# Grouped convolution ahead of a feed-forward network: 16 places in, 8 out, both parts of the weights in one stationary

## The chip, the cores and the metric

The kernel runs on one core of a Trainium2 chip. The metric is the device time of one execution in microseconds; the number given for a kernel is the median of its runs.

## The reference, cut to what matters

```
# x: 128 x 32 x 512, f32 (samples, channels, places)
out = conv_general_dilated(x, weight,          # weight: 32 x 8 x 9
        padding=[(4, 4)], feature_group_count=4)
h = out + einsum('nd,od->no', c, c_weight)[:, :, None] + bias[None, :, None]
xt = h.reshape(-1, 512)
y = (silu(xt @ W_gate.T) * (xt @ W_up.T)) @ W_down.T   # W: 1376 x 512, 512 x 1376
return x + y.reshape(x.shape)
```

The 32 channels form four groups of eight. A convolution with nine taps runs over the 512 places inside each group, and then every (sample, channel) row of 512 places goes through the gated network.

## The kernel before

**The work.** The four channel groups g = 0 to 3 are done one behind the other. For each there are two stages. The first makes gate and up for the 1376 hidden units, in eleven slices f = 0 to 10 of 128 (the last of 96), by seven products for each slice (a scheme of sums and differences of halves, so that seven take the place of eight). The second, `down`, multiplies the gated values by W_down, in 22 units for each group. f32 values are kept as two parts, hi (rounded to fp32r) and lo (the rest), and every product of two f32 matrices is three matmuls: hi by hi, lo by hi, hi by lo. A product of the first stage has two halves q of its 256 terms, so it is six matmuls of 512 columns.

**The convolution of group g + 1 runs inside the first stage of group g**, one step k = 0 to 7 for each slice (group 0's own convolution stands ahead of everything). A block is 16 places of 8 channels, 128 rows with the samples as columns; a step does four blocks, 512 columns. An output block of 16 places needs its own block of inputs and eight places of the next, so two stationaries hold the taps as banded matrices: `ta` (own block) and `tb` (the next one's part), each with hi and lo: six matmuls a step, in one PSUM bank, and ahead of them a head of three matmuls of 128 columns.

For the groups 1 to 3, which the change touches, a step goes through the engines thus (`lag(g)` is 1 for g = 0, so k = f - 1 there, and k = f later; line numbers are those of the profile):

- SyncE loads 128 places of x into `x_in` in eight transfers (L355), at k = 1, 3, 5, and at the end for the next group.
- VectorE turns 32 x 32 blocks into `x_blk` (`turn_x`, L1138), ahead of `gate_a`.
- ScalarE makes `xt_hi` (`split_x`, L859 is its helper), VectorE `xt_lo` (L1091 is its helper).
- TensorE multiplies, one iteration later and behind product 3 (`conv_step`, L640 and L645; `conv_head`, L631, behind product 1 at k = 1).
- VectorE adds `ctxb` and writes to `win` (`read_conv`, L1192; `read_head`, L1182), behind `prepare` and ahead of `up_b`.
- SyncE sends the four windows of the step from `win` to `stage` (`stage_step`, L344), in the next iteration. An even step's read waits until the two steps before it are out of `win` (`staged`).

**The order of the work is written out by hand**: each engine has its own loop over g and f, and semaphores tie them. Inside a slice TensorE goes 1, 2, 3, 4, 0 of the next slice, 5, 6 (L727). Products 0, 2, 4 and 5 collect in the same PSUM bank, so each waits until the one before has been copied by ScalarE (`copy_chain`; product 5 waits for `copied4`). Product 6 waits until VectorE has added product 3 (`up_b`, L1260), product 3 of the next slice for `up_a` (L1265), product 1 for `gate_a` (L1255). The products `gated` are L1274 and L1278.

In group 0 the weights are prepared on the way (`prepare`): TensorE transposes them (L654, L665), VectorE makes T1 and T2, differences of weights (L1164, L1168), GpSimd T3 and T4 (L522, L523), and ScalarE (L859), VectorE (L1091) and GpSimd (L530) split them into hi and lo in `ring`, from where SyncE saves them. ScalarE's queue holds `copy_chain(n, f, 4)` behind `prepare(f + 1, 2)`, the splits of T1 and T2:

```
                    if more:
                        prepare(f + 1, 1)
                    if more:
                        prepare(f + 1, 2)
                    copy_chain(n, f, 4)
```

Groups 1 to 3 load the saved weights again (L404), and there is no `prepare`.

Of the kernel before, what the change touches and what calls it, by code (L numbers as in the profile page):

```python
# [11 lines left out]
P = 128  # L12


def adaln_ffn(nc, x, cond, bias, conv_w, ctx_w, w_gate, w_up, w_down, out):
# [8 lines left out]
    WB = 4  # L24
# [77 lines left out]
    with ExitStack() as ctx:  # L102
# [24 lines left out]
        x_in = sb("x_in", [P, CG, P])  # L127
        x_blk = sb("x_blk", [P, WB, R, CG])
# [4 lines left out]
        ta_hi = sb("ta_hi", [P, P], F32R)  # L133
        ta_lo = sb("ta_lo", [P, P], F32R)
        tb_hi = sb("tb_hi", [P, P], F32R)
        tb_lo = sb("tb_lo", [P, P], F32R)
        ident = sb("ident", [P, P])

        copy0, copy2, copy4, act_a, act_b = (mix[:, n, :] for n in range(5))

# [65 lines left out]
        x_turned = sem("x_turned")  # L206
        xt_hi_done = sem("xt_hi_done")
# [88 lines left out]
        def x_place(grp, i):  # L296
            return x_first[:, i - 1] if grp == 0 and i > 0 else x_in[:]
# [13 lines left out]
        x_turn = x_blk[:, :, :, :].rearrange("n b r c -> n (b r c)")  # L311

        def x_split_from(grp, k):
            return xt_bank(grp, k)[:] if grp == 0 else x_turn
# [35 lines left out]
        def _(sp):  # L350
            def load_x(grp, i):
                if grp > 0:
                    for quad in range(NB):
                        for c in range(CQ):
                            sp.dma_start(x_in[quad * QUAD:(quad + 1) * QUAD, c::CQ, :],  # L355
                                         x[:, grp * CG + quad * CQ + c, i * P:(i + 1) * P].rearrange("(b n) l -> n b l", b=NB)
                                         ).then_inc(x_loaded, LD)
                    return
# [130 lines left out]
        def _(pool):  # L489
# [42 lines left out]

            def mix_h_first(q):
# [15 lines left out]
            pool.tensor_copy(reorder[:].rearrange("p (m r) -> p m r", r=R), ident[:].rearrange("p (r m) -> p m r", r=R)).then_inc(consts, 1)  # L549
            wrap(1)  # L550
# [4 lines left out]
            for g in range(G):  # L555
                for f in range(FC):
                    if g == 0 and f + 2 < FC:
                        wrap(f + 2)
                    if g == 0 and f + 1 < FC:
                        mix_t(f + 1)  # L560
                        mix_t_lo(f + 1)

        @block.tensor
        def _(pe):
# [56 lines left out]
            def conv_head(grp):  # L621
# [8 lines left out]
                for n, (t, v) in enumerate(terms(tb_hi, tb_lo, *xt(grp))):  # L630
                    mm = pe.matmul(conv_ps[:, 0:P], t[:], v[:, 0:P], start=n == 0, stop=n == 2)  # L631
# [187 lines left out]
            for g in range(G):  # L819
# [3 lines left out]
                for f in range(1 if g == 0 else 0, FC):  # L823
# [33 lines left out]
        def _(act):  # L857
# [3 lines left out]
            def split_toep(grp):  # L861
# [4 lines left out]
                if grp == 1:  # L866
# [3 lines left out]
                    act.wait_ge(toep_done, 3)  # L870
                hi(ta_hi[:], toep[:, grp:grp + 1, HALO:QN, :])
                hi(tb_hi[:, TB0:P], toep[:, grp:grp + 1, 0:HALO, :]).then_inc(t_hi_done, 1)

# [168 lines left out]
            for g in range(G):  # L1042
# [3 lines left out]
                for f in range(1 if g == 0 else 0, FC):  # L1046
# [7 lines left out]
                    if conv and 0 <= k < STEPS:  # L1054
# [6 lines left out]
                    silu_a(n, f)  # L1061
                    if n == 1:
# [26 lines left out]
        def _(dve):  # L1089
# [26 lines left out]
            def split_toep(grp):  # L1116
# [4 lines left out]
                if grp == 0:  # L1121
# [4 lines left out]
                    lo(t[2][:, R - HALO:, :], in_bank[0][:, 0:HALO, :], t[3][:, R - HALO:, :]).then_inc(t_lo_done, 1)  # L1126
                else:
# [3 lines left out]
            def turn_x(grp, k):  # L1131
# [5 lines left out]
                l0 = k % 2 * WB * R  # L1137
                dve.transpose(x_turn, x_in[:, :, l0:l0 + WB * R].rearrange("p m (w r) -> p w m r", r=R)).then_inc(x_turned, 1)  # L1138
# [40 lines left out]
            def read_head(grp):  # L1179
                dve.wait_ge(ctx_done, 1 if grp == 0 else 2)  # L1180
                dve.wait_ge(conv_done, CPG * grp + 1)
                dve.tensor_tensor(head[HEAD0:P, :], conv_ps[HEAD0:P, 0:P], ctxb[HEAD0:P, grp, :],  # L1182
                                  ALU.add).then_inc(conv_out, 1)

            def read_conv(grp, k):
# [8 lines left out]
                if k == STEPS - 1:  # L1194
# [3 lines left out]
                    last = dve.tensor_copy(to[HEAD0:P, JJ - 1, :], head[HEAD0:P, :])  # L1198
                last.then_inc(conv_out, 1)
# [132 lines left out]
            for g in range(G):  # L1332
                conv = g + 1 < G
                for f in range(1 if g == 0 else 0, FC):
# [3 lines left out]
                    if conv and 0 <= k < STEPS:  # L1338
# [68 lines left out]
```

## Time and profile before

| what | value |
|---|---|
| runs | 750.9 us median of 3 (750.73 to 751.24) |
| profiled execution | 751.72 us |
| its span | 749.9 us, granted clock 0.999 |
| TensorE matmul busy | 739.6 us, 99% |
| VectorE busy | 379.5 us, 51% |
| ScalarE busy | 274.4 us, 37% |
| GpSimd busy | 52.4 us, 7% |
| group 0's first stage, with the conv of group 1 | 48 to 164 us |
| first stages of groups 1 and 2, with a conv | 228 to 348 and 405 to 524 us |

The page lists the busy time of each engine, the span in 40 slices, the chain of work that ended last, and the groups of instructions. A matmul is shown with its full passage (some 390 ns for 512 columns), while the next one starts sooner, so the busy share of TensorE says little; what counts is the distance from one start to the next.

### The profile page before, as it was taken

How to read it: one execution, taken by the hardware profiler on the slowest of the kernel's cores; microseconds unless marked ns; L12 is line 12 of the kernel's file. 1: busy time of each engine (PE TensorE's matmuls, PEld its weight loads, DVE VectorE, ACT ScalarE, POOL GpSimd, SP SyncE). 2: the span in 40 equal slices, each digit the busy share in tenths (PEclk: the TensorE clock that was granted, in tenths of full speed). 3: DMA queues.
4: the chain of work that ended last, by engine and by line, in shares of the span. 5: the costliest groups of instructions: out<-in, count | busy, mean ns of one | idle time of the engine just before them, and what ended most of it. 6: DMA issues, size and time to landing. Idle time of an engine off the chain costs nothing.

```text
span 749.9 us, 10087 instructions
## 1 busy us (share of the span) xinstructions
PE 739.6 (99%) x3375; PEld 602.4 (80%) x3375; DVE 379.5 (51%) x639; ACT 274.4 (37%) x521; POOL 52.4 (7%) x88
## 2 busy tenths in 40 slices
PE   7999999999999999999999999999999999999998
PEld 6778888878888888887888888887888888887886
DVE  3896766654765454436734545443753333334224
ACT  4565655543433233234322333324431332333221
POOL 4433323210000000000000000000000000000000
PEclk9999999999999999999999999999999999999999
DMA  6496578569977677765544866866443967775413
GB/s 186 114 317 239 187 273 281 186 226 327 354 268 247 216 222 219 197 205 159 167 135 171 282 202 193 244 194 180 162 133 106 312 190 196 194 193 172 141 29 112
DMA packets 115029, 152.37 MB, mean 203 GB/s; under 512 B 12482, under 2 KB 50530, under 8 KB 114978
## 3 DMA queue, kind: packets, MB, share of 16 engines
q1 hardware_dynamic: 114496, 151.51, 64.8%
q8 instruction: 28, 0.46, 0.2%
q10 hardware_dynamic: 482, 0.21, 0.1%
q14 instruction: 23, 0.19, 0.1%
HBM read 108.95 MB, written 34.34 MB: 191 GB/s over the span
## 4 chain that ended last, share of the span: by engine, by line
PE 94%; DVE 2%; DMA 1%; SPq 1%; issue 1%; ACT 1%; POOL 0%; POOLq 0%; DVEq 0%
PE bank L727 55%; PE bank L790 32%; PE bank L645 3%; PE bank L640 3%; SPq L344 1%; PE bank L683 1%; DVE hc_lo L1091 1%; DMA x_in<-in_x 1%; PE bank L606 1%; PE bank L654 1%; PE bank L665 0%; DMA stage<-g_all 0%; DVE g_all L1294 0%; DVE ring L1091 0%; DVE g_all L1192 0%
## 5 line engine op out<-in xcount | busy, mean ns | idle before, releaser
L727 PE MATMUL bank<-hc_hi,ring 128*128 128x512 f32 (+1 forms) x1204 | 374.0, 392 | 1.0 <-issue 1.0
L727 PEld LDWEIGHTS bank<-hc_hi,ring 128*128 128x128 f32 (+1 forms) x1204 | 221.4, 185 | 50.2 <-issue 1.4
L727 PE MATMUL bank<-hc_lo,ring 128*128 128x512 f32 (+1 forms) x602 | 234.8, 390 | 0.0
L790 PE MATMUL bank<-ring,g_hi 128*128 128x512 f32 (+1 forms) x704 | 218.6, 392 | 0.0
L790 PEld LDWEIGHTS bank<-ring,g_hi 128*128 128x128 f32 (+1 forms) x704 | 131.2, 188 | 28.1 <-DVE g_lo L1091 0.8
L859 ACT ACTIVATE mix<-bank 128x512 f32<-128x512 f32 (+1 forms) x129 | 76.7, 594 | 188.0 <-PE bank L727 188.0
L790 PE MATMUL bank<-ring,g_lo 128*128 128x512 f32 (+1 forms) x352 | 137.1, 390 | 0.0
L727 PEld LDWEIGHTS bank<-hc_lo,ring 128*128 128x128 f32 (+1 forms) x602 | 111.5, 185 | 25.8
L1091 DVE TENSOR_TENSOR g_lo<-g_all,g_hi 128x512 fp32r<-128x512 f32 (+1 forms) x88 | 60.4, 689 | 88.6 <-ACT g_hi L859 88.6
L859 ACT ACTIVATE g_hi<-g_all 128x512 fp32r<-128x512 f32 (+1 forms) x88 | 55.1, 629 | 114.1 <-PE bank L790 114.0
L1265 DVE TENSOR_TENSOR mix<-bank,mix 128x512 f32<-128x512 f32 (+1 forms) x43 | 29.7, 691 | 129.4 <-PE bank L727 129.4
L790 PEld LDWEIGHTS bank<-ring,g_lo 128*128 128x128 f32 (+1 forms) x352 | 66.1, 188 | 13.9
L1260 DVE TENSOR_TENSOR mix<-bank,mix 128x512 f32<-128x512 f32 (+1 forms) x43 | 29.6, 688 | 71.1 <-ACT mix L859 71.1
L981 ACT ACTIVATE mix<-bank 128x512 f32<-128x512 f32 (+1 forms) x43 | 25.7, 598 | 43.3 <-PE bank L727 43.3
L859 ACT ACTIVATE xt_hi<-x_blk 128x512 fp32r<-128x512 f32 (+1 forms) x33 | 17.0, 540 | 65.2 <-DVE x_blk L1138 65.2
L1091 DVE TENSOR_TENSOR hc_lo<-stage,hc_hi 128x512 fp32r<-128x512 f32 x50 | 32.9, 696 | 0.9 <-ACT hc_hi L859 0.8
L1255 DVE TENSOR_TENSOR mix<-bank,mix 128x512 f32<-128x512 f32 (+1 forms) x43 | 28.9, 671 | 7.1 <-PE bank L727 4.7
L859 ACT ACTIVATE hc_hi<-stage 128x512 fp32r<-128x512 f32 x50 | 28.6, 618 | 3.2 <-DMA stage<-g_all 3.1
L1274 DVE TENSOR_TENSOR g_all<-mix 128x512 f32<-128x512 f32 (+1 forms) x43 | 29.5, 686 | 0.0
L1278 DVE TENSOR_TENSOR g_all<-mix 128x512 f32<-128x512 f32 (+1 forms) x43 | 29.3, 682 | 0.0
L1192 DVE TENSOR_TENSOR win<-bank,ctxb 128x512 f32<-128x512 f32 (+1 forms) x24 | 16.1, 671 | 25.0 <-PE bank L645 23.2
L975 ACT ACTIVATE mix<-mix 128x512 f32<-128x512 f32 (+1 forms) x43 | 26.7, 621 | 0.0
(141 smaller groups left out, 468.7 us busy)
## 6 DMA issues: line engine op xcount, KB each, us to landing
ring<-saved SPq DMA_DIRECT2D x319, 256.0 KB, 3.0
saved<-ring SPq DMA_DIRECT2D x99, 256.0 KB, 3.7
g_all<-in_x SPq DMA_DIRECT2D x32, 256.0 KB, 3.6
out_y<-g_all SPq DMA_DIRECT2D x32, 256.0 KB, 3.7
x_in<-in_x SPq DMA_DIRECT2D x96, 64.0 KB, 2.1
stage<-win SPq DMA_DIRECT2D x96, 64.0 KB, 2.9
w_nat<-in_L_ffn_W_gate SPq DMA_DIRECT2D x10, 256.0 KB, 3.4
w_nat<-in_L_ffn_W_up SPq DMA_DIRECT2D x10, 256.0 KB, 3.4
```

The costliest lines, as they stand in the source:

```text
L640: pe.matmul(bank[:], t[:], v[:, at:at + WB * P], start=n == 0, stop=False)
L727: mm = pe.matmul(bank[0:w, :], wt, hv, start=fresh and q == 0 and t == 0, stop=q == 1 and t == 2, skip_group_check=not fresh)
L790: mm = pe.matmul(acc(half, tt)[:], gs, wd, start=f == 0 and t == 0, stop=f == FC - 1 and t == 2)
L859: return act.activation(dst, src, ACT.Copy)
L975: act.activation(act_a[0:w], act_a[0:w], ACT.Silu).then_inc(silu_a_done, 1)
L981: act.activation(act_b[0:w], chain_ps[f % 2][0:w, :], ACT.Silu).then_inc(silu_b_done, 1)
L1091: return dve.tensor_tensor(dst, src, hi_part.bitcast(F32), ALU.subtract)
L1255: dve.tensor_tensor(act_a[0:w], second_ps[0:w, :], copy0[0:w], ALU.add).then_inc(gate_a_done, 1)
L1260: dve.tensor_tensor(copy4[0:w], third_ps[0:w, :], copy4[0:w], ALU.add).then_inc(up_b_done, 1)
L1265: dve.tensor_tensor(copy2[0:w], third_ps[0:w, :], copy2[0:w], ALU.add).then_inc(up_a_done, 1)
L1274: dve.tensor_tensor(g_all[0:w, f, 0, :], copy2[0:w], act_a[0:w], ALU.mult).then_inc(g_done[0], 1)
L1278: dve.tensor_tensor(g_all[0:w, f, 1, :], copy4[0:w], act_b[0:w], ALU.mult).then_inc(g_done[1], 1)
```

## The change

For groups 1 to 3 a block of 16 input places now gives only 8 output places. With 8 outputs of 8 channels, hi and lo of the band each take 64 columns of a stationary, so both fit in one: `pair_even` is hi then lo, `pair_odd` lo then hi. A matmul of it by `xt_hi` and one by `xt_lo` give all products; the result for one half of the outputs stands as two parts in the two halves of the partitions of a bank, which are added when they are read. A step of the same 64 output places needs eight input blocks, at distances of 8 places: 1024 columns, four matmuls of 512, in the two banks `conv_ps` and `xt_ps`. `x_in` gets a margin of eight places on both sides. Core of the diff:

```diff
-        x_in = sb("x_in", [P, CG, P])
-        x_blk = sb("x_blk", [P, WB, R, CG])
+        x_in = sb("x_in", [P, CG, HALO + P + HALO])
+        x_turn = sb("x_turn", [P, 2 * WB * P])
+        conv_t = sb("conv_t", [P, 4 * P], F32R)
+        PAIRED = 1
+        HALF = P // 2
+        pair_even, pair_odd = conv_t[:, 0:P], conv_t[:, HALF:HALF + P]
...
 (load_x)
+                    size = P + HALO if paired(grp) and i < KC - 1 else P
...
 (GpSimd)
+            def pad_x(grp):
+
+                pool.wait_ge(x_turned, STEPS * grp + STEPS - 2)
+                pool.memset(x_in[:, :, HALO + P:], 0.0).then_inc(x_padded, 1)
...
+                    if g + 1 < G and paired(g + 1) and f == STEPS - 1:
+                        pad_x(g + 1)
...
 (TensorE)
+                if paired(grp):
+                    for n, v in enumerate(xt(grp)):
+                        mm = pe.matmul(conv_ps[:, 0:P], pair_odd, v[:, 2 * WB * P:], start=n == 0, stop=n == 1)
...
+            def paired_step(grp, k):
+                pe.wait_ge(xt_lo_done, STEPS * grp + k + 1)
+                pe.wait_ge(conv_out, CPG * grp + k + 1)
+                for half, (bank, t) in enumerate(((conv_ps, pair_even), (xt_ps, pair_odd))):
+                    for n, v in enumerate(xt(grp)):
+                        mm = pe.matmul(bank[:], t, v[:, half * WB * P:(half + 1) * WB * P], start=n == 0, stop=n == 1)
+                mm.then_inc(conv_done, 1)
...
                     product(g, f, 2)
+                    if conv and 1 <= k <= STEPS and paired(g + 1):
+                        paired_step(g + 1, k - 1)
                     product(g, f, 3)
-                    if conv and 1 <= k <= STEPS:
+                    if conv and 1 <= k <= STEPS and not paired(g + 1):
                         conv_step(g + 1, k - 1)
...
 (ScalarE)
+            def split_pairs(grp, k):
+                act.wait_ge(conv_done, CPG * grp + (k + 1 if k > 0 else 0))
+                act.wait_ge(x_turned, STEPS * grp + k + 1)
+                last = hi(xt_hi[:, 0:2 * WB * P], x_turn[:])
...
-                    if conv and 0 <= k < STEPS:
+                    if conv and 0 <= k < STEPS and not paired(g + 1):
                         split_x(g + 1, k)
...
                     copy_chain(n, f, 2)
                     silu_a(n, f)
+                    if conv and 0 <= k < STEPS and paired(g + 1):
+                        split_pairs(g + 1, k)
...
 (VectorE, turn_x)
+                for half in range(2 if paired(grp) else 1):
+                    at = l0 + half * HALO
+                    last = dve.transpose(x_turn[:, half * WB * P:(half + 1) * WB * P],
+                                         x_in[:, :, at:at + WB * R].rearrange("p m (w r) -> p w m r", r=R))
...
+            def split_pairs(grp, k):
+                dve.wait_ge(xt_hi_done, STEPS * grp + k + 1)
+                last = lo(xt_lo[:, 0:2 * WB * P], x_turn[:], xt_hi[:, 0:2 * WB * P])
...
 (read_head)
+                    rows = slice(HEAD0 - HALF, HALF)
+                    dve.tensor_tensor(head[HEAD0:P, :], conv_ps[rows, 0:P], ctxb[rows, grp, :], ALU.add).then_inc(conv_lo_out, 1)
+                    dve.wait_ge(conv_lo_out, (2 * STEPS + 2) * (grp - PAIRED) + 1)
+                    dve.tensor_tensor(head[HEAD0:P, :], conv_ps[HEAD0:P, 0:P], head[HEAD0:P, :], ALU.add).then_inc(conv_out, 1)
...
+            def read_pairs(grp, k):
+                i = k // 2
+                if k % 2 == 0:
+                    dve.wait_ge(staged[(i - 1) % KC], STAGED * (grp if i == 0 else grp + 1))
+                dve.wait_ge(conv_done, CPG * grp + k + 2)
+                lower, upper = slice(0, HALF), slice(HALF, P)
+                halves = ((conv_ps, lower, upper), (xt_ps, upper, lower))
+                w0 = k % 2 * WB
+                to = [windows(grp, i)[mine, w0:w0 + WB, :] for _, mine, _ in halves]
+                for n, (bank, mine, other) in enumerate(halves):
+                    dve.tensor_tensor(to[n], bank[other, :].rearrange("p (w n) -> p w n", w=WB),
+                                      ctxb[other, grp:grp + 1, :].broadcast_to([HALF, WB, P]), ALU.add).then_inc(conv_lo_out, 1)
+                for n, (bank, mine, other) in enumerate(halves):
+                    dve.wait_ge(conv_lo_out, (2 * STEPS + 2) * (grp - PAIRED) + 2 * k + n + 2)
+                    last = dve.tensor_tensor(to[n], bank[mine, :].rearrange("p (w n) -> p w n", w=WB), to[n], ALU.add)
...
-                    if conv and 0 <= k < STEPS:
+                    if conv and 0 <= k < STEPS and (k == 0 or not paired(g + 1)):
                         turn_x(g + 1, k)
...
                         split_toep(g + 1)
+                    if conv and 1 <= k <= STEPS and paired(g + 1):
+                        read_pairs(g + 1, k - 1)
                     if conv and 0 <= k < STEPS:
-                        split_x(g + 1, k)
+                        (split_pairs if paired(g + 1) else split_x)(g + 1, k)
...
-                    if conv and 1 <= k <= STEPS:
+                    if conv and 1 <= k <= STEPS and not paired(g + 1):
                         read_conv(g + 1, k - 1)
                     up_b(n, f)
...
+                    if conv and 0 <= k < STEPS - 1 and paired(g + 1):
+                        turn_x(g + 1, k + 1)
                     up_a(n, f)
```

VectorE's queue in one iteration of group 0, before the change, from `turn_x` to the last `gated`. `ring` holds weights, `t_all` T1 and T2, `win` the windows of the convolution.

```order
L1138 STREAM_TRANSPOSE x_blk<-x_in 128x512 [waits xt_lo_done,x_loaded]
L1255 TENSOR_TENSOR mix<-bank,mix 128x512 [waits g_a_done,copied0,product_done1]
L1091 TENSOR_TENSOR ring<-x_gate,ring 128x256 [waits w_hi_done] x2
L1091 TENSOR_TENSOR xt_lo<-x_blk,xt_hi 128x512 [waits xt_hi_done]
L1091 TENSOR_TENSOR ring<-bank,ring 128x256 [waits w_hi_done]
L1164 TENSOR_TENSOR t_all<-bank,x_gate 128x256
L1168 TENSOR_TENSOR t_all<-bank,t_all 128x256 [waits t4_done,t1_done]
L1091 TENSOR_TENSOR ring<-t_all,ring 128x256 [waits w_hi_done] x2
L1192 TENSOR_TENSOR win<-bank,ctxb 128x512 [waits conv_done,staged0]
L1260 TENSOR_TENSOR mix<-bank,mix 128x512 [waits copied4]
L1265 TENSOR_TENSOR mix<-bank,mix 128x512 [waits product_done6]
```

The same place after the change, from `gate_a` (L1352) to `up_a` (L1362):

```order
L1352 TENSOR_TENSOR mix<-bank,mix 128x512 [waits g_a_done,copied0,product_done1]
L1141 TENSOR_TENSOR ring<-x_gate,ring 128x256 [waits w_hi_done] x2
L1287 TENSOR_TENSOR win<-bank,ctxb 64x512 [waits conv_done,staged0]
L1287 TENSOR_TENSOR win<-bank,ctxb 64x512
L1291 TENSOR_TENSOR win<-bank,win 64x512 [waits conv_lo_out] x2
L1141 TENSOR_TENSOR xt_lo<-x_turn,xt_hi 128x1024 [waits xt_hi_done]
L1141 TENSOR_TENSOR ring<-bank,ring 128x256 [waits w_hi_done]
L1234 TENSOR_TENSOR t_all<-bank,x_gate 128x256
L1238 TENSOR_TENSOR t_all<-bank,t_all 128x256 [waits t4_done,t1_done]
L1357 TENSOR_TENSOR mix<-bank,mix 128x512 [waits copied4]
L1199 STREAM_TRANSPOSE x_turn<-x_in 128x512 [waits xt_lo_done,x_loaded]
L1362 TENSOR_TENSOR mix<-bank,mix 128x512 [waits product_done6]
```

The reads of the convolution moved from behind T1 and T2 to ahead of them, and became four; the split became twice as long; the transposes (two, of which one is shown) moved from ahead of `gate_a` to between `up_b` and `up_a`, one step early.

TensorE's queue in group 0, from the end of product 4 to product 6, after the change. `product_done`, `copied4` and `up_b_done` are what the products wait for.

```order
L687 MATMUL bank<-ident,w_nat 128x128 [waits gate_kept,nat_wrapped]
L760 MATMUL bank<-hc_hi,ring 128x512 [waits silu_b_done,w_made0]
L760 MATMUL bank<-hc_hi,ring 128x512 [waits copied4,w_made5]
L698 MATMUL bank<-ident,w_nat 128x128 [waits t2_done,nat_wrapped]
L760 MATMUL bank<-hc_hi,ring 128x512 [waits up_b_done,w_made6]
```

Nothing moved here: of each product the first row is shown (0 of the next slice, 5, 6), with its waits as before. What moved on TensorE is the convolution step, from behind product 3 to ahead of it.

## Rows read from the trace of the kernel before

**Rows 1.** The page: busy time, share of the span and instructions of each engine.
```profile
PE 739.6 (99%) x3375; PEld 602.4 (80%) x3375; DVE 379.5 (51%) x639; ACT 274.4 (37%) x521; POOL 52.4 (7%) x88
```

**Rows 2.** The chain that ended last, in order of time: start us, us, what.
```profile
94.94 5.47 PE bank L727 x24
...
131.00 5.49 PE bank L727 x24
...
347.55 57.40 PE bank L790 x252
```

**Rows 3.** Timeline, group 0, f = 1: start us, us, engine, instruction [idle before].
```profile
54.53 0.42 DVE L1164 TENSOR_TENSOR t_all<-bank,x_gate 128x256 f32<-128x256 f32 x1
...
56.52 0.71 PE L727 MATMUL bank<-hc_hi,ring 128*128 128x512 f32 x2 [0.95 <-issue]
```

**Rows 4.** Timeline, group 0, f = 5: VectorE, and SyncE's windows.
```profile
96.36 0.69 DVE L1265 TENSOR_TENSOR mix<-bank,mix 128x512 f32<-128x512 f32 x1 [3.54 <-PE bank L727]
96.97 0.68 DVE L1278 TENSOR_TENSOR g_all<-mix 128x512 f32<-128x512 f32 x1
...
101.11 0.42 DVE L1091 TENSOR_TENSOR ring<-bank,ring 128x256 fp32r<-128x256 f32 x1 [0.20 <-ACT ring L859]
101.45 0.41 DVE L1164 TENSOR_TENSOR t_all<-bank,x_gate 128x256 f32<-128x256 f32 x1
101.90 0.42 DVE L1168 TENSOR_TENSOR t_all<-bank,t_all 128x256 f32<-128x256 f32 x1
...
106.23 2.49 SPq L344 DMA_DIRECT2D stage<-win  x4
```

**Rows 5.** Timeline of TensorE, group 0: starts of product 1 (f = 5), 5, next 1.
```profile
96.16 0.62 PE L727 MATMUL bank<-hc_hi,ring 128*128 128x512 f32 x2
...
105.05 0.62 PE L727 MATMUL bank<-hc_hi,ring 128*128 128x512 f32 x2
...
108.27 0.40 PE L727 MATMUL bank<-hc_hi,ring 128*128 128x512 f32 x1
```

**Rows 6.** Groups by line and form, VectorE: busy us, mean ns | idle before.
```profile
L1138 DVE STREAM_TRANSPOSE x_blk<-x_in 128x512 f32<-128x512 f32 x24 | 16.9, 705 | 0.0
L1091 DVE TENSOR_TENSOR xt_lo<-x_blk,xt_hi 128x512 fp32r<-128x512 f32 x24 | 16.5, 689 | 3.5 <-ACT xt_hi L859 3.4
...
L1192 DVE TENSOR_TENSOR win<-bank,ctxb 128x512 f32<-128x512 f32 x21 | 14.4, 687 | 19.8 <-PE bank L645 18.0 <-DMA stage<-win 1.8
...
L1091 DVE TENSOR_TENSOR xt_lo<-x_blk,xt_hi 128x128 fp32r<-128x128 f32 x9 | 2.6, 285 | 0.0
...
L1182 DVE TENSOR_TENSOR head<-bank,ctxb 32x128 f32<-32x128 f32 x4 | 1.2, 296 | 1.2 <-PE bank L631 1.1
```

**Rows 7.** Line 344, the windows issued at 262 us: ns, starts, and landing.
```profile
L344 SPq DMA_DIRECT2D stage<-win x4: 553/594/600, 261.9 to 263.8; - x4
...
DMA to landing us min/median/max: 2.7/3.0/3.3
```

**Rows 8.** The page's DMA issues, loads of x: KB each, median us to landing.
```profile
x_in<-in_x SPq DMA_DIRECT2D x96, 64.0 KB, 2.1
```

**Rows 9.** Timeline of VectorE, group 0, f = 2, around the head's read.
```profile
62.46 0.66 DVE L1255 TENSOR_TENSOR mix<-bank,mix 128x512 f32<-128x512 f32 x1
63.14 0.30 DVE L1182 TENSOR_TENSOR head<-bank,ctxb 32x128 f32<-32x128 f32 x1
63.47 0.42 DVE L1091 TENSOR_TENSOR ring<-x_gate,ring 128x256 fp32r<-128x256 f32 x1
```

**Rows 10.** Line 344, the windows issued at 106.2 us.
```profile
DMA to landing us min/median/max: 2.4/2.6/2.7
```

**Rows 11.** Timeline, group 1, step 2: start of product 1, and the read.
```profile
261.34 0.61 PE L727 MATMUL bank<-hc_hi,ring 128*128 128x512 f32 x2
...
267.07 0.69 DVE L1192 TENSOR_TENSOR win<-bank,ctxb 128x512 f32<-128x512 f32 x1 [1.56 <-PE bank L645]
```

**Rows 12.** Line 344, the windows issued at 272.8 us.
```profile
DMA to landing us min/median/max: 3.7/3.9/4.0
```

More of the change, by code:

```diff
@@ L296, in x_place @@
         def x_place(grp, i):
-            return x_first[:, i - 1] if grp == 0 and i > 0 else x_in[:]
+            return x_first[:, i - 1] if grp == 0 and i > 0 else x_in[:, :, HALO:HALO + P]
         def blocks(grp, k):
@@ L310, in adaln_ffn @@
         NB, CQ = P // QUAD, CG // (P // QUAD)
-        x_turn = x_blk[:, :, :, :].rearrange("n b r c -> n (b r c)")
         def x_split_from(grp, k):
-            return xt_bank(grp, k)[:] if grp == 0 else x_turn
+            return xt_bank(grp, k)[:] if grp == 0 else x_turn[:, 0:WB * P]
         def xt_at(grp, k):
@@ L629, in conv_head @@
                     pe.wait_ge(conv_out, CPG * grp)
-                for n, (t, v) in enumerate(terms(tb_hi, tb_lo, *xt(grp))):
-                    mm = pe.matmul(conv_ps[:, 0:P], t[:], v[:, 0:P], start=n == 0, stop=n == 2)
+                if paired(grp):
+                    for n, v in enumerate(xt(grp)):
+                        mm = pe.matmul(conv_ps[:, 0:P], pair_odd, v[:, 2 * WB * P:], start=n == 0, stop=n == 1)
+                else:
+                    for n, (t, v) in enumerate(terms(tb_hi, tb_lo, *xt(grp))):
+                        mm = pe.matmul(conv_ps[:, 0:P], t[:], v[:, 0:P], start=n == 0, stop=n == 2)
+                mm.then_inc(conv_done, 1)
[5 more added lines that the diff above has]
+                        mm = pe.matmul(bank[:], t, v[:, half * WB * P:(half + 1) * WB * P], start=n == 0, stop=n == 1)
                 mm.then_inc(conv_done, 1)
@@ L870, in split_toep @@
                     act.wait_ge(toep_done, 3)
+                if paired(grp):
+                    for at in (0, P):
+                        last = hi(conv_t[:, at:at + HALF], toep[:, grp:grp + 1, HALO:2 * HALO, :])
+                    last.then_inc(t_hi_done, 1)
+                    return
                 hi(ta_hi[:], toep[:, grp:grp + 1, HALO:QN, :])
                 hi(tb_hi[:, TB0:P], toep[:, grp:grp + 1, 0:HALO, :]).then_inc(t_hi_done, 1)
+            def split_pairs(grp, k):
+                act.wait_ge(conv_done, CPG * grp + (k + 1 if k > 0 else 0))
+                act.wait_ge(x_turned, STEPS * grp + k + 1)
+                last = hi(xt_hi[:, 0:2 * WB * P], x_turn[:])
+                if k == 0:
+                    last = hi(xt_hi[:, 2 * WB * P:], head[:])
+                last.then_inc(xt_hi_done, 1)
             def split_x(grp, k):
@@ L1198, in read_conv @@
                     last = dve.tensor_copy(to[HEAD0:P, JJ - 1, :], head[HEAD0:P, :])
+                last.then_inc(conv_out, 1)
+            def read_pairs(grp, k):
[13 more added lines that the diff above has]
+                    last = dve.tensor_tensor(to[n], bank[mine, :].rearrange("p (w n) -> p w n", w=WB), to[n], ALU.add)
+                if k == STEPS - 1:
+                    last.then_inc(conv_lo_out, 1)
+                    dve.wait_ge(conv_lo_out, (2 * STEPS + 2) * (grp - PAIRED + 1))
+                    last = dve.tensor_copy(windows(grp, i)[HEAD0:P, JJ - 1, :], head[HEAD0:P, :])
                 last.then_inc(conv_out, 1)
```

33 lines of the change are left out of this document (25 added, 8 removed).

## The prediction

> **What bounds the kernel now.** The page comes first: TensorE is busy for 739.6 of 749.9 us, VectorE for 51%, ScalarE for 37% [rows 1]. Busy matmuls are pipelined, so I look next at whether TensorE ever waits. The chain of waits in order of time is one row of products behind the other: 252 matmuls in 57.40 us, 0.228 us for each matmul of 512 columns, with no gap [rows 2]. So a product (six matmuls) takes 1.37 us, and a matmul taken away is worth 0.228 us where nothing else is late. Two stretches matter. The eight conv steps of channel group 1 run during group 0's products f = 1 to 9, where iterations are 12.0 us apart (three of them in 131.00 - 94.94 = 36.06 us [rows 2]). Those of groups 2 and 3 run during the products of groups 1 and 2, where an iteration is 48 matmuls, 10.93 us. Then I read one iteration of each kind, on VectorE, ScalarE and TensorE together. The reader should see in it what TensorE takes from VectorE: product 5 needs the copy of product 4, and that copy stands on ScalarE's queue behind the splits of T1 and T2, which VectorE makes. In f = 1 this wait already shows: T1 starts at 54.53, product 5 at 56.52 after 0.95 us of idle TensorE, so product 5 starts **1.99 us after T1** when T1 is late [rows 3]. In a normal iteration T1 starts at 101.45, so the copy would allow 103.44, and product 5 starts at 105.05, when its turn comes [rows 4, 5]. T1 has 1.6 us of slack.
>
> **What the change takes from TensorE.** Columns per group before: head 3 x 128, seven steps of 6 x 512, one of 3 x 512 + 3 x 384, together 24576. After: 2 x 128 + 32 x 512 = 16640. The difference, 7936 columns at 0.228 us per 512, is 3.53 us per group and 10.6 us in all. The page will count 17 matmuls fewer per group (51 - 34).
>
> **What it adds on VectorE**, per step. One read of 687 ns becomes four, each of 64 partitions but as many columns. A transpose of 705 ns becomes two. The split of 512 columns (689 ns) becomes one of 1024: the slope between 128 columns (285) and 512 (689) is 1.05 ns per column, so 1.23 us, and 1.14 until the next can start [rows 6]. By throughput alone that fits: about 3 us more in 11.5. What counts is the place. The four reads and the long split now stand ahead of T1, T2 and up_b; before, the one read stood behind T1 and T2. Beside other work lie:
> - the two transposes, 1.3 us between up_b and up_a, where VectorE now waits 3.54 us for product 6 [rows 4]; if that idle time went, they would cost it in full;
> - the loads they read. They are asked for in the same place of SyncE's queue, behind the four windows. In groups 1 and 2 those are issued by 3.1 us after product 1 begins; eight more issues at the windows' 0.62 end by 8.1, and landing takes 2.1 [rows 7, 8]: 10.2, just ahead of the transposes, which begin at 10.4 in those iterations by the count below;
> - ScalarE's split, of the same columns, which runs beside the reads and would have to exceed 2.7 us to hold VectorE;
> - GpSimd's four small memsets. One of them stands in f = 7 behind GpSimd's splits, and VectorE's last transposes wait for it, in the same idle time.
>
> **What a read costs.** Neighbours start 0.61 us apart although each lasts 0.69 (96.36, 96.97 [rows 4]). The new reads cross from one half of the partitions to the other, alternately, which before never does. Bounds: 0.35 if half the partitions cost half the time, 0.61 as neighbours do, 0.72 if each waits until the one in front is finished. The nearest row is the head's read, the one instruction that starts at another partition than its neighbours. It starts at 63.14, after the end of the one in front (62.46 + 0.66), and the next starts at 63.47, after its own end [rows 9]. So I take 0.69 + 0.03 = **0.72**, four reads 2.88. Against half the time speaks the head's 296 ns on 32 partitions beside 285 on 128, both of 128 columns [rows 6].
>
> The Trainium skill has a rule for this ("VectorE: DVE Perf Modes", section "Two Vector instructions with no wait between them"): an instruction whose input or output starts in another group of 32 partitions than the last one's is held until all earlier ones have finished. By that rule a read is 0.72, without it 0.61, and the sum below would be 759.6; rows 9 agree with the rule.
>
> **Group 0, one iteration**, counted from the start of product 1. Products 1 and 2 end at 2.73, the four new matmuls at 3.64. VectorE sees the end of a product 0.20 after TensorE has gone on (96.16 and 96.36 [rows 4, 5]), so the reads run from 3.84 to 6.72, the split to 7.86; one short operation (0.34, from 101.11 to 101.45 [rows 4]), and T1 starts at 8.20. Product 5 follows at 10.19. Before, it started 8.89 after product 1 (105.05 - 96.16), now it could at some 8.4. From its start to the next product 1 are 3.22 us (108.27 - 105.05 [rows 5]). So the iteration takes 13.4 us, not 12.0: **+1.4**, with the saving already in it. The others differ from it:
> - Steps 2, 4 and 6 also wait until the windows of the step before have left `win`. SyncE issues these 4.33 us after T2's start (101.90, 106.23 [rows 4]), here 0.45 before product 1 begins; the last goes 1.9 later [rows 7] and lands after 2.6 [rows 10]: near 4.1, so +0.25, in all +1.65.
> - In f = 2 the head comes first. VectorE's two adds, 0.33 each, end at 3.35; the four matmuls start at 3.40, not 2.85, and T1 at 8.86: 14.1 against 12.3 (its iteration held the head before too), +1.8.
> - f = 9 has a read but no split: 12.5 against 11.85, +0.7.
> - f = 1 has no read, but three transposes and a split of 1152 columns on both engines, T1 1.4 later; it was late already, so all of it counts: +1.4.
>
> Sum: 1.4 + 1.8 + 3 x 1.4 + 3 x 1.65 + 0.7 = **+13.0**.
>
> **Groups 1 and 2, each.** There is no T1; product 6 needs up_b. Odd steps: reads to 6.72, split to 7.86, up_b done at 8.55, and product 6 starts at 9.11 (46 matmuls less its own six): no wait. Steps 2, 4 and 6 wait for the windows. SyncE issues them behind the refills of the ring, from 261.9 to 263.8, they land 3.0 later [rows 7], and VectorE's read starts at 267.07, 5.73 after product 1 began at 261.34 [rows 11]. That was when the conv's matmuls were done anyway; now they are done 1.9 earlier and the windows are late next: 5.73 + 2.88 + 1.14 + 0.69 + 0.10 (handing over) = 10.54 against 9.11, 1.4 us of idle TensorE, three times. The head costs 0.55 as above. So -3.53 + 0.55 + 4.2 = **+1.2**, twice: +2.4.
>
> **Sum:** 13.0 + 2.4 = +15.4 on the profiled execution's 751.7. That one stands 0.8 above the median of the runs, 750.9, so the forecast is 750.9 + 15.4 = **766.3 us**, slower.
>
> **Rivals.**
> - *Neighbours' pitch:* the reads cost 0.61. Reads and split together are then 0.48 shorter, eight times in group 0 and six times later, 6.7 us: 759.6. Rows 9 speak against it.
> - *The other side, cheap half reads:* at 0.35 four reads take 1.4 and T1 starts at 6.72, product 5 at 8.71, an iteration 11.9 against 12.0. Group 0: 1.4 + 0.3 - 0.3 + 0.45 - 0.5 = +1.3. Later up_b is done at 9.06, before 9.11: -3.0 per group. In all -4.7: 746.2, faster. It decides from where four reads take less than about 1.9 us. The head's 296 ns speak against it; that no row shows 64 partitions, for it.
> - *Late windows:* one burst of the same transfers landed after 3.9 [rows 12]. If all six of groups 1 and 2 do, each costs 0.9 more: +5.4, 771.7. For it: the moved timing meets other refills. Against: one of group 1's seven bursts did it, by the same view.
> - *All hidden:* only the matmuls count, 740.3. It would need the reads to stand behind T1, and they don't.
>
> **How the numbers follow.** The forecast's own case gets 0.60 (761 to 770: 0.3 us either way in each of 14 waits), neighbours' pitch 0.22, late windows 0.11, cheap reads or all hidden 0.05, a wash 0.02. The likeliest gives 766.3; the range 757 to 772 takes in the second and third case. A measurement here tells 0.2%, 1.5 us, from no change: faster 0.05, same 0.02, slower 0.93.
>
> **What would show it.** TensorE idle ahead of product 5 in f = 1 to 9 (1.5 to 2 us each) and ahead of product 6 in three iterations of groups 1 and 2; T1 near 8.2; iterations of 13.4 and 13.65; the reads 0.72 apart. Reads 0.35 or 0.61 apart, T1 before 6.4, or no idle time ahead of product 6 would prove that step wrong. The whole fails if VectorE's queue is short of work where I count it full.

## The result and the profile after

| what | before | after |
|---|---|---|
| median of the runs beside each other | 751.07 us (6 runs, 750.32 to 751.78) | 770.51 us (6 runs, 769.15 to 773.53) |
| profiled execution, its span | 751.72, 749.9 us | 770.19, 768.2 us |

The ratio is 1.026, with an interval of 1.0246 to 1.0274: slower, by 19.4 us where 15.4 were forecast. The time lies inside the range of 757 to 772.

The page of the changed kernel, busy times, the slices of two engines, and the groups on VectorE (out<-in, count | busy us, mean ns | idle before, and for what); they answer to [rows 1, 6]:

```profile
PE 732.9 (95%) x3324; PEld 593.8 (77%) x3324; DVE 458.6 (60%) x729; ACT 282.2 (37%) x515; POOL 52.3 (7%) x92
...
PE   8988878889999999999999999999999999999998
...
DVE  4897888865485777763854678764663333334224
...
L1287 DVE TENSOR_TENSOR win<-bank,ctxb 64x512 f32<-64x512 f32 x48 | 33.1, 689 | 28.1 <-DMA stage<-win 14.4
...
L1291 DVE TENSOR_TENSOR win<-bank,win 64x512 f32<-64x512 f32 x48 | 33.1, 689 | 1.1
L1141 DVE TENSOR_TENSOR xt_lo<-x_turn,xt_hi 128x1024 fp32r<-128x1024 f32 x24 | 29.4, 1226 | 6.7 <-ACT xt_hi L894 6.1
```

TensorE has its 51 matmuls fewer (3375 - 3324) and is busy for 95% of the span, not 99%. A slice is 19.2 us; but for the last one, the slices below 9 stand in the first 173 us, where group 0's first stage is. VectorE is 79 us busier. The reader should compare 33.1 + 33.1 us for the reads with the 14.4 of one read a step (21 of 24 steps) [rows 6]: a read of 64 partitions takes 689 ns, as one of 128 did (687).

What TensorE now waits for, from the view of waits (engine, line, what for: us in total, times, longest):

```profile
PE bank L760 <- ACT mix L894: 15.4, 8, 2.1
PE bank L760 <- DVE mix L1357: 6.2, 6, 1.3
PE bank L760 <- issue: 2.6, 1, 2.6
...
PE bank L664 <- DVE head L1256: 1.7, 3, 0.6
```

Three of the forecast's waits stand here in order. Product 5 waits for ScalarE's copy in f = 2 to 9, eight times, and in f = 1 once more (the 2.6 that the view puts down to issue). Product 6 waits for `up_b` six times, in groups 1 and 2. The conv's matmuls wait three times for the head. Together 25.9 us, of which only the 0.95 of f = 1 was there before [rows 3].

VectorE in one iteration of group 0, f = 3, whose product 1 starts on TensorE at 77.48 (timeline: start us, us, engine, instruction, idle before):

```profile
79.70 0.69 DVE L1352 TENSOR_TENSOR mix<-bank,mix 128x512 f32<-128x512 f32 x1
80.31 0.75 DVE L1141 TENSOR_TENSOR ring<-x_gate,ring 128x256 fp32r<-128x256 f32 x2
81.32 1.41 DVE L1287 TENSOR_TENSOR win<-bank,ctxb 64x512 f32<-64x512 f32 x2 [0.26 <-PE bank L664]
82.76 1.39 DVE L1291 TENSOR_TENSOR win<-bank,win 64x512 f32<-64x512 f32 x2
84.18 1.23 DVE L1141 TENSOR_TENSOR xt_lo<-x_turn,xt_hi 128x1024 fp32r<-128x1024 f32 x1
85.44 0.42 DVE L1141 TENSOR_TENSOR ring<-bank,ring 128x256 fp32r<-128x256 f32 x1
85.78 0.41 DVE L1234 TENSOR_TENSOR t_all<-bank,x_gate 128x256 f32<-128x256 f32 x1
```

and TensorE, where product 1 starts, where product 5 starts, and where the next product 1 does:

```profile
77.48 0.62 PE L760 MATMUL bank<-hc_hi,ring 128*128 128x512 f32 x2
...
87.82 0.70 PE L760 MATMUL bank<-hc_hi,ring 128*128 128x512 f32 x2 [1.98 <-ACT mix L894]
...
91.11 0.62 PE L760 MATMUL bank<-hc_hi,ring 128*128 128x512 f32 x2
```

Counted from product 1: reads at 3.84, split at 6.70, T1 at 8.30, product 5 at 10.34. Four reads take 84.18 - 81.32 = 2.86 us. The next product 1 starts at 91.11, after 13.63 us.

Group 1, step 2, whose product 1 starts at 277.68, on VectorE:

```profile
283.26 1.41 DVE L1287 TENSOR_TENSOR win<-bank,ctxb 64x512 f32<-64x512 f32 x2 [2.66 <-DMA stage<-win]
284.70 1.39 DVE L1291 TENSOR_TENSOR win<-bank,win 64x512 f32<-64x512 f32 x2
286.12 1.23 DVE L1141 TENSOR_TENSOR xt_lo<-x_turn,xt_hi 128x1024 fp32r<-128x1024 f32 x1
287.38 0.69 DVE L1357 TENSOR_TENSOR mix<-bank,mix 128x512 f32<-128x512 f32 x1
```

on TensorE:

```profile
288.22 0.70 PE L760 MATMUL bank<-hc_hi,ring 128*128 128x512 f32 x2 [1.30 <-DVE mix L1357]
```

and the burst of windows that the read waits for, by line 356 (instructions, durations in ns, first and last start), where the answering rows are [rows 7]:

```profile
L356 SPq DMA_DIRECT2D stage<-win x4: 552/595/600, 278.2 to 280.1; - x4
...
DMA to landing us min/median/max: 3.1/3.2/3.5
```

The last window, issued at 280.1, lands some 3.2 later, and the read starts at 283.26, 5.58 after product 1. Product 6 starts 10.54 after it. That this is the forecast's number to the hundredth is luck: the read started 0.15 earlier than counted (5.58 for 5.73), and `up_b` 0.12 later behind the split (1.26 for 1.14). Of the six such waits this is the longest, 1.30 us; the six are 1.04 on average.

### Where the time went

`up_a` closes an iteration on VectorE. The distances between its starts, before and after:

| iteration | before | after | more | forecast |
|---|---|---|---|---|
| group 0, up to f = 1 | 60.02 | 62.91 | 2.9 | 1.4 |
| f = 2 | 12.33 | 14.77 | 2.4 | 1.8 |
| f = 3 to 8, mean of six | 11.97 | 13.66 | 1.7 | 1.4 and 1.65 |
| f = 9 | 10.79 | 11.91 | 1.1 | 0.7 |
| group 1 in all | 169.65 | 170.58 | 0.9 | 1.2 |
| group 2 in all | 176.57 | 177.35 | 0.8 | 1.2 |

Group 0 lost 16.6 us (166.91 to 183.51), groups 1 and 2 together 1.7: 18.3, the difference of the spans. The runs say 19.4: the execution profiled before stood 0.7 above its median and the one after 0.3 below.

The theory for the experiments is the prediction's: in group 0 the reads and the long split stand ahead of T1 on VectorE, and TensorE waits for what hangs on T1; in groups 1 and 2 the windows leave `win` too late. Rivals to be told apart: that VectorE and the DMA queues carry too much, wherever it stands; that the transfers in group 0 (SyncE saves weights there) hold it; and, for the reads, that their crossing from one half of the partitions to the other costs nothing.

### The profile page after: what moved, and what is told of

Read it like the earlier page. It is cut to its first block, busy times and chain, and to the rows that moved or that the text cites. A ratio compares the mean times of both kernels' runs of the same rounds, so it can differ in the third digit from the quotient of the medians.

```text
span 768.2 us, 10073 instructions
## 1 busy us (share of the span) xinstructions
PE 732.9 (95%) x3324; PEld 593.8 (77%) x3324; DVE 458.6 (60%) x729; ACT 282.2 (37%) x515; POOL 52.3 (7%) x92
## 4 chain that ended last, share of the span: by engine, by line
PE 78%; DVE 11%; DMA 3%; issue 3%; SPq 2%; ACT 2%; POOL 0%; DVEq 0%; ACTq 0%; POOLq 0%
PE bank L760 42%; PE bank L823 31%; DVE win L1287 3%; PE bank L664 2%; DMA stage<-win 2%; DVE xt_lo L1141 2%; SPq L356 2%; DVE win L1291 2%; DVE ring L1141 1%; ACT mix L894 1%; PE bank L716 1%; ACT ring L894 1%; DVE hc_lo L1141 1%; DMA x_in<-in_x 1%; DVE mix L1357 1%
## 5 line engine op out<-in xcount | busy, mean ns | idle before, releaser
L760 PE MATMUL bank<-hc_hi,ring 128*128 128x512 f32 (+1 forms) x1204 | 375.6, 393 | 24.3 <-ACT mix L894 15.4
L1362 DVE TENSOR_TENSOR mix<-bank,mix 128x512 f32<-128x512 f32 (+1 forms) x43 | 29.7, 690 | 85.2 <-PE bank L760 85.2
L1287 DVE TENSOR_TENSOR win<-bank,ctxb 64x512 f32<-64x512 f32 x48 | 33.1, 689 | 28.1 <-DMA stage<-win 14.4
L1352 DVE TENSOR_TENSOR mix<-bank,mix 128x512 f32<-128x512 f32 (+1 forms) x43 | 29.7, 690 | 8.3 <-PE bank L760 3.1
L1291 DVE TENSOR_TENSOR win<-bank,win 64x512 f32<-64x512 f32 x48 | 33.1, 689 | 1.1
L1141 DVE TENSOR_TENSOR xt_lo<-x_turn,xt_hi 128x1024 fp32r<-128x1024 f32 x24 | 29.4, 1226 | 6.7 <-ACT xt_hi L894 6.1
L894 ACT ACTIVATE ring<-t_all 128x256 fp32r<-128x256 f32 (+1 forms) x44 | 18.0, 413 | 38.9 <-DVE t_all L1234 31.7
L1199 DVE STREAM_TRANSPOSE x_turn<-x_in 128x512 f32<-128x512 f32 x48 | 30.9, 682 | 1.6 <-POOL x_in L549 1.6
```

Of the source, the lines that this page charges most:

```text
L760: mm = pe.matmul(bank[0:w, :], wt, hv, start=fresh and q == 0 and t == 0, stop=q == 1 and t == 2, skip_group_check=not fresh)
L894: return act.activation(dst, src, ACT.Copy)
L1141: return dve.tensor_tensor(dst, src, hi_part.bitcast(F32), ALU.subtract)
L1199: last = dve.transpose(x_turn[:, half * WB * P:(half + 1) * WB * P], x_in[:, :, at:at + WB * R].rearrange("p m (w r) -> p w m r", r=R))
L1287: dve.tensor_tensor(to[n], bank[other, :].rearrange("p (w n) -> p w n", w=WB), ctxb[other, grp:grp + 1, :].broadcast_to([HALF, WB, P]), AL ...
L1291: last = dve.tensor_tensor(to[n], bank[mine, :].rearrange("p (w n) -> p w n", w=WB), to[n], ALU.add)
```

## Experiments

**1. The new convolution for groups 2 and 3 alone, and for group 1 alone.** The places of the loss, apart.

```diff
-        PAIRED = 1
+        PAIRED = 2
```

> The new convolution for groups 2 and 3 alone; group 1's, which runs inside group 0's products, stays as before. If the loss comes from T1 standing behind the reads in group 0 (my theory, 16.6 us of the 18.3 between the two profiles), only the waits ahead of product 6 and the heads remain: 751.1 + 1.7 = 752.8 us (752 to 754). If the loss is simply VectorE's added work, wherever it stands, two thirds of 19.4 us remain: 764 us.

```diff
-            return grp >= PAIRED
+            return grp == PAIRED
```

> The complement: the new convolution for group 1 alone, groups 2 and 3 as before. T1's place: 751.1 + 16.6 = 767.7 us (766 to 770), with TensorE idle ahead of product 5 in f = 1 to 9. Added work wherever it stands: one third of 19.4, 757.5 us.

The first ran in 752.7 us (10 runs, ratio 1.0019, 1.0008 to 1.003), the second in 768.95 (1.0231, 1.0216 to 1.0247). The two excesses over the 751.5 before, 1.2 and 17.4, add up to 18.6 beside the 19.4 of both parts together. So nine tenths of the loss are made in group 0's first stage, and the parts do not act on each other much. (The kernel before, run again beside each set of experiments, took 751.05 to 751.53 us; differences between kernels of different sets are good to about 0.5 us.)

**2. The windows earlier.** SyncE sends the windows of step k one iteration later, ahead of the refills of the ring. Here they go out in the same iteration, behind the fifth refill, in the kernel of experiment 1 whose groups 2 and 3 have the new convolution. The same move in the kernel before is its control.

```diff
-                    if g + 1 < G and k == 2:
+                    if g + 1 < G and k == 1:
...
-                    if g + 1 < G and 2 <= k < STEPS + 2:
-                        stage_step(g + 1, k - 2)
...
-                    for fk in phase1[7 * f + 1:7 * f + 8]:
+                    for nth, fk in enumerate(phase1[7 * f + 1:7 * f + 8]):
+                        if nth == 4 and g + 1 < G and 1 <= k < STEPS + 1:
+                            stage_step(g + 1, k - 1)
```

> As e1_late_groups, and SyncE issues a step's windows in the same iteration, behind the refill for the next slice's product 0, not in the next iteration behind those for products 5 and 6. If the late windows hold the reads of steps 2, 4 and 6, these now start 3.8 us after product 1, product 6 never waits, and groups 1 and 2 each gain 3.53 - 0.55: 751.1 - 6.0 = 745.1 us (744 to 747). If product 6 is late because of VectorE's amount of work, nothing changes against e1: 753 us.

> Control: the same earlier issue of the windows in the kernel before. There the reads were not held by the windows by more than 0.1 us, and nothing waited for them: no change, 751.1 us within 1 us. If the earlier transfers are worth something by themselves (or disturb the refills), it shows here.

With the new convolution it ran in 745.02 us (0.9909, 0.9895 to 0.9924), 7.7 less than without the move. The kernel before did not change: 751.45 (0.9995, 0.9985 to 1.0004). Odd and even iterations of the new steps now take the same time; VectorE's timeline of one in group 1:

```profile
271.78 0.69 DVE L1362 TENSOR_TENSOR mix<-bank,mix 128x512 f32<-128x512 f32 x1 [0.71 <-PE bank L760]
...
275.42 1.41 DVE L1287 TENSOR_TENSOR win<-bank,ctxb 64x512 f32<-64x512 f32 x2 [0.92 <-PE bank L664]
...
282.22 0.69 DVE L1362 TENSOR_TENSOR mix<-bank,mix 128x512 f32<-128x512 f32 x1 [0.78 <-PE bank L760]
```

The read waits for TensorE's matmuls, not for a transfer, and the iteration takes 10.44 us. So the wait for the windows did cost nearly what was counted (7.7 us where 3 x 1.4 a group make 8.4), the matmuls taken away are worth their full price once it is gone, and before the change the same transfers were hidden, with some 0.3 us to spare (the last issued at 263.8, landed 3.0 later, the read at 267.07 [rows 7, 11]).

**3. T1 first.** In group 0, from f = 2 on, T1 and T2 and the short split in front of them go ahead of the reads on VectorE. ScalarE's part of that short split goes ahead of its long split likewise. The amount of work is the same.

```diff
 (ScalarE, and the same ahead of read_pairs on VectorE)
+                    if more and k >= 1:
+                        prepare(f + 1, 1)
...
-                    if more:
+                    if more and k < 1:
                         prepare(f + 1, 1)
```

> The changed kernel with T1 and T2 (and the short split ahead of them) moved to ahead of the four reads, for f = 2 to 9; the reads and the long split still stand ahead of up_b. My theory: the wait leaves product 5 and comes back ahead of product 6, since up_b is done only near 11.6 us after product 1: iterations of 13.1 instead of 13.7, 766 us (764 to 768), TensorE idle ahead of product 6, not 5. If the wait is for VectorE's amount of work, the time stays at 770.5.

764.32 us (1.0179, 1.0161 to 1.0198): 6.2 less, 1.7 beyond what was expected, which is about the fall of the clock below, absent in its profile. An iteration takes 13.05 to 13.1 instead of 13.66. The wait ahead of product 5 is gone from f = 2 on, and another has taken its place; `up_b` in f = 3 (timeline of VectorE):

```profile
86.70 0.69 DVE L1359 TENSOR_TENSOR mix<-bank,mix 128x512 f32<-128x512 f32 x1
```

and TensorE's product 6:

```profile
87.54 0.70 PE L760 MATMUL bank<-hc_hi,ring 128*128 128x512 f32 x2 [1.45 <-DVE mix L1359]
```

This is the next in line: `up_b` (L1359), now behind reads, split and the splits of T1 and T2, holds product 6 by 1.45 us.

**4. T1, T2 and then `up_b` first.** As experiment 3 for every f, and with `up_b` ahead of the splits of T1 and T2 on VectorE. T1 reuses a buffer whose readers must be done, for which it got two waits.

```diff
+                    if f > 0:
+                        dve.wait_ge(w_made[K_S1], f)
+                        dve.wait_ge(w_made[K_S2], f)
...
                     up_b(n, f)
+                    if more:
+                        prepare(f + 1, 2)
```

> The changed kernel with T1 and T2 ahead of the reads for all f, ScalarE's split for them ahead as well, and up_b ahead of the two splits of T1 and T2. Counted through, T1 starts near 3.7, up_b ends at 9.2, before product 6's turn at 10.0, and the iteration is bound by VectorE's own row of work, some 11.6 us: 2.05 us less in seven iterations, 1 in f = 9, 2.5 in f = 1: 752.6 us (751 to 756). If order does not matter: 770.5.

751.89 us (10 runs, 1.0004, 0.9994 to 1.0013): as the kernel before, and 18.6 less than the change. The same instructions, as many transfers, only in another order: so neither the amount of VectorE's work nor the traffic of group 0 makes the 16.6 us. TensorE's waits:

```profile
PE bank L760 <- DVE mix L1360: 6.6, 7, 1.1
...
PE bank L760 <- issue: 1.6, 2, 1.3
```

Nothing waits for ScalarE's copy any more. In group 0 a single product waits from f = 3 on, product 6 of f = 7, for 0.23 us (of the 6.6; the other six waits are those of groups 1 and 2). What is left above 745 is the windows' wait of groups 1 and 2, as in experiment 1.

**5. Reads that all start at the same partition.** Each of the four reads takes all 128 partitions of its bank, straight across. The semaphores and the order stay.

```diff
-                    dve.tensor_tensor(to[n], bank[other, :].rearrange("p (w n) -> p w n", w=WB),
+                    dve.tensor_tensor(to[n], bank[:].rearrange("p (w n) -> p w n", w=WB),
...
-                    last = dve.tensor_tensor(to[n], bank[mine, :].rearrange("p (w n) -> p w n", w=WB), to[n], ALU.add)
+                    last = dve.tensor_tensor(to[n], bank[:].rearrange("p (w n) -> p w n", w=WB), to[n], ALU.add)
```

> The changed kernel, but its four reads take all 128 partitions straight across and write the second bank's sum to an unused place, so that consecutive reads start at the same partition; each has as many columns as before. Left out: the adding of the two halves, so the convolution of groups 1 to 3 is not computed. If reads are 0.72 apart because they change halves: 0.61 apart here, some 0.45 us less in eight iterations and in six later waits, 764 us (763 to 766). If they are 0.72 apart because of their semaphores or their PSUM banks: no change, 770.5.

761.33 us (1.0131, 1.0116 to 1.0146), 9.2 less than the change. VectorE in f = 3, as above:

```profile
79.49 0.69 DVE L1287 TENSOR_TENSOR win<-bank,ctxb 128x512 f32<-128x512 f32 x1 [0.26 <-PE bank L664]
80.09 0.68 DVE L1287 TENSOR_TENSOR g_all<-bank,ctxb 128x512 f32<-128x512 f32 x1
80.69 0.68 DVE L1291 TENSOR_TENSOR win<-bank,win 128x512 f32<-128x512 f32 x1
81.29 0.68 DVE L1291 TENSOR_TENSOR g_all<-bank,g_all 128x512 f32<-128x512 f32 x1
81.89 1.22 DVE L1141 TENSOR_TENSOR xt_lo<-x_turn,xt_hi 128x1024 fp32r<-128x1024 f32 x1
83.02 0.42 DVE L1141 TENSOR_TENSOR ring<-bank,ring 128x256 fp32r<-128x256 f32 x1
```

The reads start 0.60 us apart instead of 0.72 though each moves twice the data and lasts as long, and behind the split the next starts after 1.13 instead of 1.26. Together 0.6 an iteration, and iterations are 13.05 instead of 13.66: seven times in group 0, and 0.3 in f = 9, which has no long split, 4.5 us. In groups 1 and 2 the waits of product 6 fell from 6.2 to 3.4 us. Of the rest, 1.9, up to 1.3 is the clock's fall again, which this kernel's profile does not have: `up_a` of f = 1 starts at 61.65 instead of 62.91. So the price taken for a read holds, and the cheap half read is excluded: 64 partitions cost what 128 cost. It is not the crossing of one read that costs the 0.12. The two reads of L1291 add within their own half, and they too are 0.71 apart in the changed kernel (84.18 - 82.76, halved). What all four have in common there, and none here, is that something they read or write starts at another partition than in the instruction in front; and since semaphores and banks are the same in both kernels, they are not the cause.

**6. Both repairs.** Experiments 4 and 2 in one kernel, and once more beside the next experiment, on the same chip.

```diff
-                    if g + 1 < G and k == 2:
+                    if g + 1 < G and k == 1:
...
                     up_b(n, f)
+                    if more:
+                        prepare(f + 1, 2)
```

> e6_t1_upb_first with the windows issued early as in e3: the waits ahead of product 6 in groups 1 and 2 go too, 7.7 us less than e6: 745 us (743 to 748), the best of the kernels here with e3 if group 0's iterations are really near 11.6 us. If group 0 is bound by VectorE at 12 us or more, it is no better than e3.

> e8 unchanged, as the neighbour of e10 on the same chip: 744.8 us. It also tells how often TensorE's clock falls: if a fall costs about 1.6 us and comes from waits of over 2 us, which this kernel has none of in group 0, its clock is 1.00 again.

744.80 us (0.9909, 0.9894 to 0.9924) and 744.38 (0.9906, 0.9891 to 0.9921). The repairs add: 7.1 less than experiment 4. But the runs show no gain over the kernel of experiment 2 that leaves group 1 with the old convolution: 744.80 and 744.38 beside 745.02, ratios of 0.9909 and 0.9906 beside 0.9909. Between the profiles it is 1.0 (spans of 743.8 and 742.8). VectorE in group 0 shows why, its timeline from one `up_a` to the next, nearly without a gap:

```profile
84.88 0.68 DVE L1365 TENSOR_TENSOR mix<-bank,mix 128x512 f32<-128x512 f32 x1
...
89.67 1.41 DVE L1290 TENSOR_TENSOR win<-bank,ctxb 64x512 f32<-64x512 f32 x2 [0.29 <-DMA stage<-win]
...
95.35 1.30 DVE L1199 STREAM_TRANSPOSE x_turn<-x_in 128x512 f32<-128x512 f32 x2
96.57 0.69 DVE L1365 TENSOR_TENSOR mix<-bank,mix 128x512 f32<-128x512 f32 x1
```

11.69 us an iteration, against 11.97 before: in group 0 VectorE's amount of work is the bound now. It leaves 0.28 us of the 0.46 that TensorE no longer does in a step, and the waits of f = 1 (0.84 and 0.35) and of the head (0.79) take part of that back. TensorE's granted clock was 0.999 or 1.000 in all eight runs, as expected of a kernel without a long wait there.

**7. The head's wait moved.** Every step multiplies into `xt_ps` first, which the head does not use, and step 0 waits for the head's read only ahead of `conv_ps`.

```diff
-                for half, (bank, t) in enumerate(((conv_ps, pair_even), (xt_ps, pair_odd))):
+                order = ((1, xt_ps, pair_odd), (0, conv_ps, pair_even))
+                for nth, (half, bank, t) in enumerate(order):
+                    if k > 0 or nth == 1:
+                        pe.wait_ge(conv_out, CPG * grp + k + 1)
```

> e8, but step 0 of each group does the two matmuls of the bank that the head does not use first, and waits for VectorE's read of the head only ahead of the other two. I priced the head at 0.55 us of idle TensorE per group; 0.46 of it would now be covered by matmuls, three times: 1.4 us less, 743.4 us (743 to 744.3, group 0's share may be lost where VectorE binds). If the idle time ahead of step 0 is covered by slack later in the iteration: no change, 744.8.

742.90 us (0.9888, 0.9872 to 0.9905), 1.5 less than experiment 6 on the same chip. The line for the head, three times and 1.9 us in all, is gone from TensorE's waits ahead of the conv's matmuls. This is the fastest kernel of the study, 1.1% below the one before.

## Why the prediction was right, and its sizes short

**The mechanism held, step by step.** *The place on VectorE* (reads and split ahead of T1, product 5 two us behind T1): T1 at 8.30, product 5 at 10.34; experiments 3 and 4 take the loss away by order alone. *The price of a read*, 0.72: measured 0.72, and experiment 5 shows that 0.12 of it comes from the change of the starting partition between neighbours. *The windows*: product 6 at up to 10.54, by experiment 2 worth 7.7 us in two groups. *The head*, 0.55: waits of 0.56 to 0.58, and experiment 7 gives 1.5 back. *The matmuls*, 3.53 a group: iterations of 10.44 for 10.93. No rival came about. The time alone would have misled here: 770.5 lies just above the 761 to 770 that the forecast gave its own case, and nearest to the 771.7 of the rival of late windows. But none of the six bursts of windows that a read waited for landed later than 3.5 us after its issue (medians of 2.8 to 3.2, as the forecast's 3.0, not the rival's 3.9), and the late groups cost less than forecast, not more. Neighbours' pitch is what experiment 5 builds, at 0.60 and 761.3 us; the change does not run like it. The last transposes did wait for GpSimd's memset, 1.61 us at 144.99, in VectorE's idle time as the forecast had it, but `up_a` started at 146.22 right behind them: no slack was left. It cost nothing yet: f = 7 and 8 together took 27.26 us, twice 13.63.

**The step that was mis-sized is group 0's sum**, 13.0 where the profiles show 16.6.

- *T1 at 8.20 and 13.4 an iteration.* Measured 8.3 to 8.4 and 13.66. The instruction behind the split started 1.26 after it, not 1.14; product 5 came 2.04 after T1, not 1.99, and the next product 1 3.29 after that, not 3.22. Each is small, but all stand on one path: 0.22 together, in every iteration from f = 3 to 8. I had applied the delay of a change of halves to the reads and the split, and not to the first instruction behind them that reads PSUM again. The rule cited in the prediction says it, in the Trainium skill, "VectorE: DVE Perf Modes", section "Two Vector instructions with no wait between them": the start is compared for each memory with the last instruction that read from it. The split reads SBUF alone, so the last read of PSUM is the fourth read's, from partition 64, and the small split behind it starts at partition 0. The trace agrees: 1.26 in the change, 1.13 in experiment 5, where all start at 0.
- *Late windows in the even steps*, 0.25 each: did not come. All eight first reads of group 0 waited for TensorE and none for a transfer. That over-pricing hid part of the first error, by luck: 1.4 and 1.65 forecast, 1.5 to 1.85 measured.
- *f = 2*, 1.8: 2.4. The head's second add ended 3.57 us after product 1, not 3.35, its iteration began with VectorE late, and T1 stood at 9.45 (72.16 - 62.71), not 8.86. *f = 9*, 0.7: 1.1. The prediction gives its terms as one number, so which of them was short stays open.
- *f = 1*, 1.4: 2.9, of which 1.6 are no wait at all but TensorE's clock. This term was missing altogether.
- *Groups 1 and 2*, 2.4: 1.7. The six waits cost less than 1.4 each.

Sum of the misses in the profiles: 1.6 for the clock, 1.0 for f = 3 to 8, 0.6 for f = 2, 0.4 for f = 9, less 0.1 for the rest of f = 1 and 0.7 for the late groups: 2.8 of the 2.9 us between 18.3 and 15.4.

## What to carry to other kernels

Work added to a queue that is handled in order is priced by what stands behind it: find the one instruction that another engine is waiting for, and see how much slack it had. Before a step is made shorter, look for the transfer that was only just hidden behind it, and send it as soon as its data is there. The amount of added work sets the time only once the order is right.

## What the runs showed of the hardware that I had not expected

**The clock fell after a wait, in some executions.** TensorE in the changed kernel, f = 1, products 5 and 6 and what lies between (timeline):

```profile
57.83 0.70 PE L760 MATMUL bank<-hc_hi,ring 128*128 128x512 f32 x2 [2.64 <-issue]
...
59.58 1.05 PE L698 MATMUL bank<-ident,w_nat 128*128 128x128 f32 x4
60.28 1.20 PE L760 MATMUL bank<-hc_hi,ring 128*128 128x512 f32 x2
```

and the same stretch in the view of windows (us, busy us of PE, PEld, DVE, ACT, POOL, then the granted clock, DMA share, GB/s):

```profile
57.80:62.70 4.90, 4.87 (x16) 3.96 (x17) 2.12 (x4) 3.13 (x7) 2.55 (x6) 0.65 0.71 243
...
60.00:62.00 2.00, 2.00 (x7) 1.71 (x7) 0.00 (x0) 1.62 (x4) 0.35 (x3) 0.50 0.83 281
```

A pair of matmuls that lasts 0.62 takes 1.20. From 59 to 62 us the granted clock is 0.50, the lower level, 1.2 GHz; up to 58 and from 64 on it is 1.00. What TensorE did before was to stand idle for 2.64 us and then to multiply at the full clock for some 1.2. From product 5 to the next product 1 it took 4.88 us instead of 3.3: 1.6 us lost. Group 1 alone (experiment 1) has the same idle time in f = 1 without a fall there, and a fall behind the next wait, in f = 2 (timeline of TensorE):

```profile
72.50 0.70 PE L760 MATMUL bank<-hc_hi,ring 128*128 128x512 f32 x2 [2.02 <-ACT mix L894]
```

Its granted clock is 0.66 in the 5 us behind that wait:

```profile
72.50:77.50 5.00, 5.00 (x17) 4.08 (x18) 2.04 (x4) 3.14 (x7) 2.47 (x5) 0.66 0.66 234
```

Experiments 3 and 5 idle for some 2.65 us in f = 1 too, and their profiles show 1.00 behind it. The other runs hint at falls too: over the span the granted clock was 0.995 to 0.998 in the six runs of the changed kernel and 0.993 to 0.998 in the four of group 1 alone. In the profiles of both, TensorE waits eight times for about 2.0 us or more (1.97 to 2.65) in group 0's first stage. In every run of the kernel before beside the experiments, of the late groups of experiment 1, and of experiments 2, 4, 6 and 7 it was 0.999 or 1.000, and in their profiles no wait of a first stage exceeds 1.6 us. So a wait here can cost 1.6 us more than its length, and whether it does is not settled by the wait's length alone; what else decides stays open.

**A transfer's place matters more than its landing time.** The windows land in about 3 us at either place in SyncE's queue (medians of 2.7 in the changed kernel and 2.9 with the move); experiment 2 gained 7.7 us by asking for them earlier.
